# Eight flags as bits of one word, and the positive parts of two Newton rounds taken by ScalarE

## What is computed

```
scores = einsum('bhqd,bhkd->bhqk', qh, kh) * 32 ** -0.5
# sparsemax: tau is such that sum(max(scores - tau, 0)) = 1 in each row
attn = clip(scores - tau, 0)
x = x + (einsum('bhqk,bhkd->bhqd', attn, vh) -> rows) @ Wo + bo
real, imag = xn @ cos(theta + theta_noise), xn @ sin(phi + phi_noise)
x = x + sqrt(real * real + imag * imag)
```

## Time and profile before

| | |
|---|---|
| median of 3 runs | 723.84 us (723.6 to 726.55) |
| the profiled execution | 725.45 us, its span 723.7 us |
| TensorE busy | 584.8 us (81% of the span) |
| VectorE busy | 609.3 us (84%) |
| ScalarE busy | 380.7 us (53%) |
| GpSimd busy | 187.1 us (26%) |
| mean granted clock of TensorE | 0.902 of full speed |

### The profile page before, as it was taken

How to read it: one execution, slowest core, us unless ns; L and a number is a source line. 1 busy time by engine, 2 the same in 40 slices (tenths; PEclk the granted TensorE clock), 3 DMA queues, 4 the chain that set the end, 5 groups by cost and what they waited for, 6 DMA issues and landing times.

```text
span 723.7 us, 14347 instructions
## 1 busy us (share of the span) xinstructions
PE 584.8 (81%) x4560; PEld 332.5 (46%) x4560; DVE 609.3 (84%) x2964; ACT 380.7 (53%) x657; POOL 187.1 (26%) x239
## 2 busy tenths in 40 slices
PE   3785989798814998899899998990889988997575
PEld 1343545454402654565455544550445544655242
DVE  5699799977966999999999999994899999999600
ACT  3664565766611755666566646560456665563321
POOL 2511403241220240415033502351014430301301
PEclk9879978999965999999999999996899999996857
DMA  9752131202220113130303030303102111200000
GB/s 315 237 166 72 27 103 47 59 0 71 68 76 0 28 28 101 33 84 15 110 26 95 6 105 28 106 1 84 42 1 78 39 45 31 59 17 14 11 1 11
DMA packets 33471, 44.23 MB, mean 61 GB/s; under 512 B 8353, under 2 KB 26785, under 8 KB 33382
## 3 DMA queue, kind: packets, MB, share of 16 engines
q1 hardware_dynamic: 32332, 41.16, 20.0%
q10 hardware_dynamic: 1056, 2.10, 0.8%
HBM read 23.77 MB, written 1.64 MB: 35 GB/s over the span
## 4 chain that ended last, share of the span: by engine, by line
PE 64%; issue 16%; ACT 11%; DVE 4%; SPq 3%; DMA 1%; POOL 1%; POOLq 0%; DVEq 0%
PE ring L456 33%; PE ring L522 8%; PE ring L545 5%; PE ring L599 5%; PE mix_bank L570 5%; PE ring L495 4%; PE ring L507 3%; ACT qst L674 2%; ACT S L674 2%; SPq L248 2%; ACT ctx L674 1%; DMA S<-in_L_xattn_Wk 1%; SPq L252 1%; ACT v L674 1%; ACT ks L682 1%
## 5 line engine op out<-in xcount | busy, mean ns | idle before, releaser
L929 DVE MAX8 cand<-S 100x8 f32<-100x45 f32 (+1 forms) x2048 | 223.1, 188 | 0.5 <-issue 0.4
L456 PE MATMUL ring<-wv,ctx 128*121 128x512 f16 x576 | 156.7, 392 | 0.0
L456 PE MATMUL ring<-ctx,wk 128*128 128x361 f16 x768 | 136.1, 339 | 4.5 <-DVE ctx L1108 4.5
L798 ACT ACTIVATE pT<-ring 121x800 f32<-121x800 f32 x96 | 80.5, 839 | 75.2 <-PE ring L599 75.2
L674 ACT ACTIVATE S<-ring 100x722 f32<-100x722 f32 x128 | 95.2, 774 | 27.6 <-PE ring L545 27.2
L456 PEld LDWEIGHTS ring<-ctx,wk 128*128 128x128 f16 x768 | 78.9, 104 | 58.6 <-issue 14.9
L333 POOL TENSOR_TENSOR ctx<-ctx_f,ctx 128x484 f16<-128x484 f32 x42 | 50.6, 1205 | 163.8 <-ACT ctx L674 163.4
L545 PE MATMUL ring<-kst,qst 96*100 96x361 f16 x256 | 68.0, 361 | 29.4 <-ACT S L674 12.9
L456 PEld LDWEIGHTS ring<-wv,ctx 128*121 128x121 f16 x576 | 71.8, 137 | 33.4 <-issue 7.9
L599 PEld LDWEIGHTS ring<-qst,kst 99*121 99x121 f16 x768 | 61.5, 150 | 45.5 <-issue 21.7
L341 POOL TENSOR_TENSOR ks<-k_f,ks 128x361 f16<-128x361 f32 x64 | 57.2, 894 | 90.9 <-ACT k_f L686 88.2
(11 more groups left out here) (126 smaller groups left out, 727.3 us busy)
## 6 DMA issues: line engine op xcount, KB each, us to landing
kst<-ks SPq DMA_DIRECT2D x384, 45.1 KB, 1.9
ctx_f<-in_ctx SPq DMA_DIRECT2D x45, 242.0 KB, 2.9
xq<-in_x SPq DMA_DIRECT2D x8, 200.0 KB
xr<-in_x SPq DMA_DIRECT2D x8, 200.0 KB
out_y<-att SPq DMA_DIRECT2D x8, 200.0 KB
S<-in_L_xattn_Wk ACTq DMA_DIRECT2D x1, 1024.0 KB, 6.8
wq<-in_L_xattn_Wq ACTq DMA_DIRECT2D x1, 1024.0 KB, 11.3
wcos<-in_L_ffn_theta SPq DMA_DIRECT2D x1, 1024.0 KB, 10.4
```

What stands on the lines that cost most here:

```text
L456: last = nc.tensor.matmul(psum, lhs(c, i), w(c, j), start=(c == 0 and n == 0), stop=(c == DC - 1 and n == 2))
L798: nc.scalar.activation(pT[0:CK, u % 3, :, :], src, ACT.Relu).then_inc(two_read, 1)
L929: last = nc.vector.max(cand[:, h, 8 * n:8 * n + 8], S[0:L, HH * (i % 2) + h, cuts[n]:cuts[n + 1]])
```

## The change

Three things change. First, in Newton rounds three and four of every unit but the first, the positive part of the difference is taken by ScalarE (`positive`), with one semaphore to it and one back, while VectorE folds and counts the masks; VectorE sums the differences after the reciprocal. Second, the last count is no longer made on VectorE: it writes one mask of 8 ranks in 16 pieces, and TensorE sums it over the rows with 8 matmuls of 128 columns more (`minus` for ranks 1 to 7, plus for rank 8), while one of the two old ones goes. VectorE sums 17 numbers for each head out of the accumulator. Third, the marked heads are no longer ranked; their marks are added as powers of two to one word, and the refining loop tests one bit in each of 8 turns, without a load in a turn. The last Newton step is held at zero or above.

```diff
@@ TensorE
             def sum_flags(i):
                 pe.wait_ge(flag_ready, i + 1)
                 if i > 0:
                     pe.wait_ge(aT_ready, 2 * i)
-                nc.tensor.matmul(flag_ps, ones[:, :], n_over[:, :], start=True, stop=False)
-                nc.tensor.matmul(flag_ps, minus[:, :], n_now[:, :], start=False, stop=True).then_inc(flag_sum, 1)
+                marks = over[:, :, :].rearrange("p g (n r) -> p g n r", r=8)
+                nc.tensor.matmul(flag_ps[:, :, PIECES], ones[:, :], n_over[:, :], start=True, stop=True)
+                for r in range(8):
+                    last = nc.tensor.matmul(flag_ps[:, :, 0:PIECES], (one_b if r == 7 else minus_b)[:, :],
+                                            marks[:, :, :, r], start=(r == 0), stop=(r == 7))
+                last.then_inc(flag_sum, 1)
@@ ScalarE
+            def positive(i, turn):
+                if 0 < i < NH:
+                    dif_now = dif[:, :, 0:PIECES * RANKS[turn]]
+                    act.wait_ge(mask_ready, relu_use(i, turn))
+                    nc.scalar.activation(dif_now, dif_now, ACT.Relu).then_inc(relu_ready, 1)
...
                     run(units, 2)
+                    positive(i, 2)
                     if 0 <= b - 1 < B:
                         square(b - 1, 0)
                     run(units, 1)
+                    positive(i, 3)
                     if b + 1 < B:
                         qT_of(b + 1)
...
                     run(units, 2)
                     if 0 < b < B:
                         v_of(b, 2)
+                    positive(i, 2)
                     run(units, 2)
                     if 0 < b < B:
                         v_of(b, 3)
                     run(units, 1)
+                    positive(i, 3)
@@ VectorE, thresholds
-                    n_mask = counted(nc.vector.tensor_scalar(over[:, :, 0:E], dif[:, :, 0:E], 0.0, None, ALU.is_ge))
-                    n_dif = counted(nc.vector.tensor_scalar(dif[:, :, 0:E], dif[:, :, 0:E], 0.0, None, ALU.max))
-                    after(n_mask)
+                    shared = i > 0 and turn >= 2
+                    mask = nc.vector.tensor_scalar(over[:, :, 0:E], dif[:, :, 0:E], 0.0, None, ALU.is_ge)
+                    if shared:
+                        mask.then_inc(mask_ready, 1)
+                        dve.wait_ge(mask_ready, relu_use(i, turn))
...
                     n = counted(nc.vector.reciprocal(step_t[:, :], n_over[:, :]))
+                    if shared:
+                        dve.wait_ge(relu_ready, relu_use(i, turn))
+                        n = counted(nc.vector.reduce_sum(f_sum[:, :], dif[:, :, 0:E], AX))
...
-                counted(nc.vector.tensor_tensor(marks[:, :, :, 7:8], pieces[:, :, :, 7:8],
-                                                t4.broadcast_to([L, HH, PIECES, 1]), ALU.is_lt))
-                n = counted(nc.vector.tensor_tensor(marks[:, :, :, 0:7], pieces[:, :, :, 0:7],
-                                                    t4.broadcast_to([L, HH, PIECES, 7]), ALU.is_ge))
-                after(n)
-                n = counted(nc.vector.tensor_tensor(fold[:, :, 2:2 + NCAND // 2], over[:, :, 0:NCAND // 2],
-                                                    over[:, :, NCAND // 2:NCAND], ALU.add))
-                after(n)
-                n = counted(nc.vector.reduce_sum(n_now[:, :], fold[:, :, :], AX))
-                after(n)
-                nc.vector.scalar_tensor_tensor(n_now[:, :], n_now[:, :], -float(PIECES), n_over[:, :],
-                                               ALU.add, ALU.min).then_inc(flag_ready, 1)
+                nc.vector.tensor_tensor(marks, pieces, t4.broadcast_to([L, HH, PIECES, 8]), ALU.is_ge).then_inc(flag_ready, 1)
@@ VectorE, flags
+                nc.vector.reduce_sum(lost[:, :], flag_ps, AX).then_inc(check_step, 1)
+                dve.wait_ge(check_step, 1)
+                nc.vector.scalar_tensor_tensor(code[:, :], lost[:, :], 0.5, bit_c[:, :],
                                                ALU.is_gt, ALU.mult).then_inc(check_step, 1)
-                nc.vector.max(ranked[:, :], code[:, :]).then_inc(check_step, 1)
-                nc.vector.tensor_copy(ranked_i[:, :], ranked[:, :]).then_inc(check_step, 1)
+                    nc.vector.reduce_sum(word_i[:, :], code[:, :], AX).then_inc(check_step, 1)
...
-                    with dve.Fori(0, HH // 2) as pair:
-                        leading = dve.value_load(ranked_i[0:1, bass.ds(2 * pair, 1)], min_val=0, max_val=HH)
-                        with dve.If(leading > 0):
-                            with dve.Fori(0, 2) as k:
-                                number = dve.value_load(ranked_i[0:1, bass.ds(2 * pair + k, 1)], min_val=0, max_val=HH)
-                                with dve.If(number > 0):
-                                    refine(i, number)
+                    with dve.Fori(0, HH) as h:
+                        with dve.If(((word >> h) & 1) > 0):
+                            refine(i, h)
```

More of the change, by code:

```diff
@@ L148, in build_kernel @@
         dif, over = sb("dif", [L, HH, NCAND]), sb("over", [L, HH, NCAND], BF16)
-        fold = sb("fold", [L, HH, 2 + NCAND // 2], BF16)
+        fold = sb("fold", [L, HH, 2 + PIECES * max(RANKS) // 2], BF16)
         tau = sb("tau", [L, 2, HH])
[L151 to L154, removed]
+        f_sum, step_t, n_over = (sb(n, [L, HH]) for n in ("f_sum", "step_t", "n_over"))
+        zero = sb("zero", [L, 1])
+        one_b, minus_b = sb("one_b", [L, 1], BF16), sb("minus_b", [L, 1], BF16)
+        bit_c, code, lost = (sb(n, [1, HH]) for n in ("bit_c", "code", "lost"))
+        word_i = sb("word_i", [1, 1], I32)
         again, againT = sb("again", [P, 32]), sb("againT", [P, 32])
@@ L211, in st_unit, with relu_use @@
             return (KC // 2) * (2 * i + g) + c
+        def relu_use(i, turn):
+            return 2 * (i - 1) + turn - 1
         block = es.enter_context(nc.Block())
@@ L927, in maxes @@
                 dve.wait_ge(two_read, seen2(("s", i, h)))
+                if h == 0 and i > 0:
+                    dve.wait_ge(flag_ready, i)
                 for n in range(PIECES):
@@ L947, in thresholds @@
                     after(n)
-                    n_mask = counted(nc.vector.tensor_scalar(over[:, :, 0:E], dif[:, :, 0:E], 0.0, None, ALU.is_ge))
-                    n_dif = counted(nc.vector.tensor_scalar(dif[:, :, 0:E], dif[:, :, 0:E], 0.0, None, ALU.max))
-                    after(n_mask)
+                    shared = i > 0 and turn >= 2
[3 more added lines that the diff above has]
+                        dve.wait_ge(mask_ready, relu_use(i, turn))
+                    else:
+                        n_mask = counted(mask)
+                        n_dif = counted(nc.vector.tensor_scalar(dif[:, :, 0:E], dif[:, :, 0:E], 0.0, None, ALU.max))
+                        after(n_mask)
                     n_fold = counted(nc.vector.tensor_tensor(fold[:, :, 2:2 + E // 2], over[:, :, 0:E // 2],
                                                              over[:, :, E // 2:E], ALU.add))
-                    after(n_dif)
-                    counted(nc.vector.reduce_sum(f_sum[:, :], dif[:, :, 0:E], AX))
+                    if not shared:
+                        after(n_dif)
+                        counted(nc.vector.reduce_sum(f_sum[:, :], dif[:, :, 0:E], AX))
                     after(n_fold)
@@ L1012, in test_sums, with refine @@
                 dve.wait_ge(fix, 3 + P // 32)
[L1014 to L1018, removed]
+            def refine(i, h):
+                t = tau[:, i % 2, bass.ds(h, 1)]
+                row = S[0:L, bass.ds(h + HH * (i % 2), 1), :].rearrange("p a n -> p (a n)")
                 dve.sem_clear(fix)
@@ L1045, in split_again, with read_flags @@
                 dve.wait_ge(fix, 5)
-            def rank_flags(i):
+            def read_flags(i):
                 dve.sem_clear(check_step)
                 dve.wait_ge(flag_sum, i + 1)
-                nc.vector.scalar_tensor_tensor(code[:, :], flag_ps, 0.5, order_c[:, :],
+                nc.vector.reduce_sum(lost[:, :], flag_ps, AX).then_inc(check_step, 1)
+                dve.wait_ge(check_step, 1)
+                nc.vector.scalar_tensor_tensor(code[:, :], lost[:, :], 0.5, bit_c[:, :],
                                                ALU.is_gt, ALU.mult).then_inc(check_step, 1)
-                dve.wait_ge(check_step, 1)
-                nc.vector.max(ranked[:, :], code[:, :]).then_inc(check_step, 1)
                 dve.wait_ge(check_step, 2)
-                nc.vector.tensor_copy(ranked_i[:, :], ranked[:, :]).then_inc(check_step, 1)
+                with nc.allow_low_precision(reason="a sum of distinct powers of two under 256"):
+                    nc.vector.reduce_sum(word_i[:, :], code[:, :], AX).then_inc(check_step, 1)
             def settle(i):
                 dve.wait_ge(check_step, 3)
-                first = dve.value_load(ranked_i[0:1, 0:1], min_val=0, max_val=HH)
-                with dve.If(first < 1):
```

(16 more changed lines are left out.)

16 lines of the change are left out of this document (9 added, 7 removed).

## The result

The changed kernel takes 775.64 us (median of 4 runs, 774.48 to 776.18), the kernel before 724.79. The ratio is 1.0697, its 95% interval 1.0668 to 1.0727. It is 51 us slower, where 15 were forecast. The direction was right and so were most of the places; the size was not, and the range of 724 to 747 does not hold it.

The account below looks back on a forecast made before the run. In mid-run TensorE and ScalarE, handing accumulators to each other, were taken to set the pace, with VectorE the follower. Terms of 26.4 us up and 11.8 down gave +14.6, so 738 us; range 724 to 747.

Parts of the forecast that it names:

- Eight are 0.5 us by that ... +0.4 us in each of 16 phases, 6.4 us.: Count sums on TensorE: eight small matmuls, less the one that goes, add 0.4 us a phase; at worst double.
- Odd phases, +1.5 us, bounds 0.8 and 3.0.: ScalarE waits 1.6 us for the round-four mask, so q transposed begins 1.5 us later; six odd phases cost 9.0.
- Even phases, +0.95 us.: ScalarE's round-three positive part delays the first aT, +0.8 us; the round-four one delays the first score eviction, +0.15.
- Phases 1 and 4.: q transposed begins 3.2 us later in phase 1; VectorE is late after refining in phase 4, 3.0 us in all.
- The whole term of the positive parts: ScalarE's positive parts in rounds three and four: odd phases 9.0, phase 1 3.2, even phases 4.8, phase 4 3.0 us.
- Down: 11.8: All savings: refining of unit 3 2.5 and unit 10 1.3, loop 2.2 and 3.2, last unit 2.6 us.
- The loop term: Refining loop with eight bit-test turns at 0.45 us saves 2.2 and 3.2 us; bounds nothing and 4 each.
- the flags were to come 2.5 us sooner: Refining of unit 3: VectorE would already be waiting for TensorE's sums, then need some 0.65 us: -2.5 us.
- The last unit's 2.6 us: VectorE's saved work on positive parts, fold and count counts only in the last unit, where TensorE waits: -2.6 us.
- The clock, a rival with 0.14.: The new wait makes TensorE's clock fall more often, 10 us on top in seven pairs: 748 us; chance 0.14.
- the forecast's own signs: TensorE waits 2 us for q transposed, over 1 for aT; pair about 78, sums 0.4 to 0.6, refining 2 shorter.
- The new work on ScalarE is hidden: Rival: both positive parts fall into ScalarE's 29.5 idle us of 75, leaving -5.4: 718 us; chance 0.14.

Follow-up runs that it names:

- step4: The changed kernel with masks laid in pairs of ranks, so TensorE reads numbers 4 bytes apart, not 16, and VectorE writes them in four instructions: 755.5 us.
- positive_only: The kernel before with one part of the change: ScalarE takes the positive parts of rounds three and four; 748.8 us, ratio 1.0328.
- positive_even: The kernel before with ScalarE taking the positive parts of rounds three and four in even phases alone: 743.4 us, ratio 1.0257.
- sums_step4: The changed kernel without the positive parts on ScalarE and with mask numbers 4 bytes apart for TensorE: 727.2 us, ratio 1.003.
- word_only: The kernel before with one part of the change: the word of marks and the refining loop with a bit test, no ranking; 725.6 us, ratio 1.0009.
- last_unit: The kernel before with positive parts on ScalarE and the last count on TensorE in the last unit alone, numbers 4 bytes apart: 725.0 us, ratio 1.0.
- no_positive: The changed kernel, but VectorE takes all positive parts itself, as before; sums on TensorE and the word stay: 754.9 us, ratio 1.0401.
- later_places: positive_only with both positive parts one place later on ScalarE, behind the first aT and a pT or behind q transposed: 737.0 us, ratio 1.0168.

## Why the prediction was wrong

*"Eight are 0.5 us by that ... +0.4 us in each of 16 phases, 6.4 us."* This is the term that failed. It measured 1.77 us a phase, 28 in all. The row it came from has adjacent f16 numbers, and here they are 16 bytes apart. The price in the Trainium skill (TensorE: Matmul & The Clock Gate, Back-to-back issue gap) that I had weighed against the row, 81 ns a matmul, lies between the 58 ns measured for adjacent numbers and the 223 ns for these, and would not have held the time either. I had noted that no row prices this and took double as the worst; it was four times. step4 gives the same eight at 0.45 and the kernel 20 us back. The bound was the fault: nothing in the rows excluded more than double, and the range was cut where I had no row. It was even narrower than its own bounds: 738 plus 6.4 for the sums, 9 for six odd phases at 3.0 and 5.4 for the loop is 759, not 746. That would not have held 776 either.

Of the 36 us between the 15 forecast and the 51 measured, this term is 22. Savings that did not come are some 7, and the positive parts 4; both are below.

*Odd phases, +1.5 us, bounds 0.8 and 3.0.* Right as far as it was worked out: ScalarE's 1.51 us of idle and TensorE's 1.98 at q transposed are in the trace. positive_only has 1.1 to 1.7 in phases 5, 7 and 9, but 3.3 in phase 3 and 2.7 in phase 13, which the forecast took for the same.

*Even phases, +0.95 us.* 0.75 was measured from phase 6 on, the push of the first `aT` and nothing for the scores; phase 2 cost 2.0. That VectorE would be early enough held in the changed kernel; positive_even shows what it is worth when it does not.

*Phases 1 and 4.* Forecast 3.2 and 3.05 for the positive parts. positive_only has 2.7 and, with the first refining in the same distance, 4.4. The whole term of the positive parts was 20 us, and it measured 24.

*"Down: 11.8".* Most of it did not come. In sums_step4, which has all the savings but the positive parts of the last unit and has the sums at about the forecast's price, the net is +2.5 us where the same terms gave 6.4 - 11.8 = -5.4. With 0.45 us in each of 16 phases, some 5 us were saved. The loop term counted the turns behind the last refined head, and those are cheaper. It left out the turns that step over unmarked heads ahead of a marked one: the old loop jumped from rank to rank, with 2.43 us of idle between the two heads of unit 3, and the new one has 3.90. In the changed kernel the refining is 2.9 us shorter with one head and 0.7 longer with two, in word_only 0.6 longer and 0.2 shorter. Ahead of unit 10's head the same turns have 4.50 us of idle in one trace and 7.70 in the other; why is open. For the refining of unit 3 the flags were to come 2.5 us sooner after TensorE's sums; the sums themselves took 1.8 of it. The last unit's 2.6 us were not found in last_unit.

*The clock, a rival with 0.14.* It happened beside the forecast case, not in its place: two falls in a pair in three pairs, each second one worth 1.4 us. In mid-run no_positive has none of these second falls and positive_only one; step4 has them again, with phases 7 and 9 each 4.9 us longer than before. By the rule of the Trainium skill (TensorE: Matmul & The Clock Gate, A second HAM failure mode), that frequent short idle times make the clock fall and rise, it should come in every pair; the trace has it in some.

The sum by runs, in one order: sums_step4 is 2.5 us over before, the positive parts on top of it (step4) 28, and the distance of 16 bytes on top of both (the changed kernel) 20. The parts do not simply add. The positive parts cost 24 us on the kernel before, 28 on sums_step4 and 21 on the slow sums of no_positive. The distance of 16 bytes costs 28 us without the positive parts (754.9 against 727.2) and 20 with them. So the two overlap by some 7 us, and there are 4 that the positive parts cost only beside sums on TensorE. No run shows where these 4 come from. The clock does not tell the cases apart: its mean is 0.884 to 0.895 in the runs of positive_only and 0.883 to 0.894 in those of step4.

By the forecast's own signs the two waits came as described (1.98 us for q transposed, 1.11 for `aT`). The sums, the length of the pair and the refining of unit 3 did not.

"The new work on ScalarE is hidden" was wrong for the reason given: 29.5 idle us of 75 say nothing of the two places where another engine waits for the next instruction. later_places halves the cost by moving two instructions.

## What to carry to other kernels

Where two engines follow each other closely, look for who waits, not who is busy: relieving the busy follower gave it some 100 us more of waiting and the kernel no time. An instruction handed to an engine with room costs what stands behind it in that engine's order, plus the wait for its own input; choose the place for both. And price an operand's layout on the engine that reads it and on the one that writes it before moving work: if no row has that distance, leave the bound open.

## What the chip showed that I had not expected

- TensorE reading a bf16 moving operand of 128 columns, with one column of weights: 0.06 us a matmul with numbers adjacent or 4 bytes apart, 0.11 at 8 bytes, 0.22 at 16.
- VectorE comparing 1024 f32 numbers a partition into bf16: 1.22 us with both in order, 2.00 reading 32 bytes apart, 4.73 writing 256 bytes apart.
- A wait of TensorE of 2 us ahead of a thin stretch of work was followed by a second fall of the clock in some pairs of phases and not in others, with the same instructions.
